# A gated cross-attention and expert program on one core: the 16-head attention's input made in the cross-attention's tail, with one scale for both norms

## The reference

```
x = x + tanh(g_ffn[0])   * L0_ffn(layernorm(x))            # experts: adds per tile
x = x + tanh(g_xattn[1]) * L1_xattn(layernorm(x), ctx)     # rms_norm of q and k
x = x + tanh(g_ffn[1])   * L1_ffn(layernorm(x))

def L1_ffn(x):                                  # x is the LayerNorm of the rows
    h = x * rsqrt(mean(x*x) + 1e-6) * ln1_w     # a second norm on top of it
    q, k, v = h @ wq, h @ wk, h @ wv            # 16 heads of 128
    x = x + softmax(causal(q k^T / sqrt(128))) v @ wo
    ...
```

## Time and profile before

| | |
|---|---|
| median of three runs | 819.42 us |
| profiled execution | 822.67 us, span 820.9 us |
| mean granted clock of TensorE | 0.963 |
| busy, share of the span | PE 93%, PEld 76%, DVE 52%, ACT 43%, POOL 28% |
| chain that ended last | PE 81%, ACT 6%, DVE 4%, DMA 3%, POOL 2%, issue 2% |

### The profile page before, as it was taken

The page is one execution under the profiler, slowest core; times in us unless marked ns, Lnnn a source line. Parts: engine busy times, 40 slices in busy tenths (PEclk is TensorE's granted clock), DMA queues, the critical chain, the costliest instruction groups (busy, mean ns, idle before and its releaser), DMA issues.

```text
span 820.9 us, 13560 instructions
## 1 busy us (share of the span) xinstructions
PE 761.7 (93%) x4626; PEld 621.6 (76%) x4627; DVE 430.3 (52%) x831; ACT 352.7 (43%) x852; POOL 231.1 (28%) x284
## 2 busy tenths in 40 slices
PE   7998899999849985999999999999898999999996
PEld 5887755666537863898898898898686888888885
DVE  6688262111446876345445435436545566656564
ACT  3887302222137874445445455455542233333332
POOL 5110040000355425221321321310423334343430
PEclk9999789999968998999999999999989999999999
DMA  8960031111100002101100110000113334343421
GB/s 318 420 232 2 1 103 46 45 46 37 53 19 2 2 2 76 41 20 34 45 26 32 34 36 32 25 14 1 58 39 91 98 109 118 105 122 101 130 74 51
DMA packets 25670, 58.29 MB, mean 71 GB/s; under 512 B 3600, under 2 KB 14480, under 8 KB 24352
## 3 DMA queue, kind: packets, MB, share of 16 engines
q1 hardware_dynamic: 24864, 55.68, 21.0%
q0 software_dynamic: 768, 2.10, 0.8%
HBM read 51.67 MB, written 6.09 MB: 70 GB/s over the span
## 4 chain that ended last, share of the span: by engine, by line
PE 81%; ACT 6%; DVE 4%; DMA 3%; POOL 2%; issue 2%; POOLq 0%; SPq 0%; PEldq 0%; ACTq 0%; PEld 0%; DVEq 0%
PE PS L329 15%; PE PS L331 15%; PE PS L330 15%; PE PS L1374 7%; PE PS L1099 6%; PE PS L1114 3%; PE PS L441 3%; PE PS L432 2%; PE PS L399 2%; PE PS L405 2%; PE PS L1380 2%; ACT x_probT L523 1%; PE PS L387 1%; ACT x_prob L552 1%; PE PS L454 1%
## 5 line engine op out<-in xcount | busy, mean ns | idle before, releaser
L329 PE MATMUL PS<-tTh,wh 128*128 128x512 f32 x200 | 79.9, 399 | 0.0
L889 ACT ACTIVATE hhh<-hh 128x512 fp32r<-128x512 f32 x50 | 31.6, 632 | 112.2 <-DVE hh L915 100.6
L330 PE MATMUL PS<-tTl,wh 128*128 128x512 f32 x200 | 79.3, 397 | 0.0
L331 PE MATMUL PS<-tTh,wl 128*128 128x512 f32 x200 | 79.3, 397 | 0.0
L513 DVE TENSOR_TENSOR hhl<-hh,hhh 128x512 fp32r<-128x512 f32 x50 | 52.6, 1052 | 34.9 <-ACT hhh L889 34.9
L1481 ACT ACTIVATE sm<-sm,nmx 128x128 f32<-128x128 f32 x128 | 49.7, 391 | 37.5 <-DVE nmx L1538 37.5
L971 POOL TENSOR_TENSOR wl<-wraw,wh 128x512 fp32r<-128x512 f32 (+1 forms) x50 | 58.2, 1163 | 8.4 <-POOL wh L969 7.9
L513 DVE TENSOR_TENSOR oTl<-PS,oTh 128x512 fp32r<-128x512 f32 x32 | 22.1, 692 | 71.6 <-ACT oTh L1475 71.6
L969 POOL CAST wh<-wraw 128x512 fp32r<-128x512 f32 (+1 forms) x50 | 26.1, 521 | 118.2 <-PE PS L331 113.3
L1577 POOL CAST ah<-araw 128x512 fp32r<-128x512 f32 (+1 forms) x32 | 16.6, 518 | 145.0 <-PE PS L331 143.1
L1099 PE MATMUL PS<-WE,xsT 128*128 x120 | 56.4, 594 | 0.1
(11 more groups left out here) (241 smaller groups left out, 1848.4 us busy)
## 6 DMA issues: line engine op xcount, KB each, us to landing
WE<-moe SPq DMA_DIRECT2D x8, 1536.0 KB, 13.8
wraw<-moe SPq DMA_DIRECT2D x25, 384.0 KB, 3.1
araw<-attn SPq DMA_DIRECT2D x16, 384.0 KB, 3.1
cwb<-cw_d SPq DMA_DIRECT2D x20, 256.0 KB, 3.8
...
```

What stands on the lines that cost most here:

```text
L329: nc.tensor.matmul(out, wh_, xh_, start=first, stop=False, **kw)
L330: nc.tensor.matmul(out, wh_, xl_, start=False, stop=False, **kw)
L331: return nc.tensor.matmul(out, wl_, xh_, start=False, stop=last, **kw)
L889: nc.scalar.activation(hhh[half][:, :], hh[half][:, :], ACT.Copy).then_inc(s.hi_done, 1)
```

## The change

The two norms become one scale. With v the variance of a row, LayerNorm and RMSNorm together give (x - mean) divided by the root of v (1 + 1e-6) + 1e-6 x 1e-5. VectorE makes that number per tile (`input_moments`) for tiles 0 to 5, 6 and 7, GpSimd its power (`input_power`), VectorE scales X straight into FX (`input_rows`), and the weight ln1, now laid along partitions, is applied where ScalarE writes tTh and VectorE tTl (`input_high`, `input_low`, two operations of 128x128 each). tT is not written there. The turns use the four banks of the scores once they are free.

These pieces go into steps 6 to 8 of the cross-attention; the barrier between the two stages is gone, and so are the fillers and the squares. The weights of the attention have SBUF of their own now, beside the cross-attention's, and are loaded once the experts' last product is done; head 0's are split by GpSimd in the tail. The first projections and value products come in another order. Z is made by GpSimd, all eight tiles behind the split for head 1.

At the opening of cross-attention 1 the query biases move ahead of the key products of the expert stage, the ln3 power of tiles 0 and 1 goes between the fourth and sixth gathers, VectorE writes the normalised rows 0 and 1 between the last adds of expert rows, and ScalarE masks keys 0 and 1.

The diff, cut (constants, semaphores, the other buffers that move with araw, the copies of the ring's new order, the barriers of the other engines and the host's packing of ln1 are left out):

```diff
...
+        araw = [sb(f"araw{i}", [P, 3 * D], where=l1) for i in range(2)]
...
                     scores(n + 1)
                 if has(n - 1):
                     values_columns(n - 1)
+                if L and n == B:
+                    input_turn(pe, MOST)
...
                         values(n)
                     if has(n + 2):
                         query_squares(n + 2)
+                    if n == B - 1:
+                        for b in range(4):
+                            input_turn(pe, b)
                     if has(n):
                         values_back(n)
+                    if n == B - 1:
+                        for b in range(4, MOST):
+                            input_turn(pe, b)
...
 
             act.wait_ge(bias_done, 1 + L)
             if L:
+
+                for b in range(2):
+                    act.wait_ge(Es.kt_free, b + 1)
+                    for odd in range(2):
+                        m = nc.scalar.activation(m_.k2T[b][:, :, odd, :], K1[:, b, :].rearrange("p (c s) -> p c s", c=C), ACT.Copy, scale=pair_rows[:, odd:odd + 1])
+                    m.then_inc(s.keys_done, 1)
                 key_columns(act, MOST, B)
...
                     copy("oT", n, m_.oT[:, :, :].rearrange("p k s -> p (k s)"), 4 * S)
                 if has(n + 2):
                     queries(n + 2)
+                if L and n == B - 1:
+                    input_high(act, 0)
+                    input_high(act, 1)
                 if has(n) and L:
                     copy("oT", n, m_.oT[:, :, :].rearrange("p k s -> p (k s)"), 4 * S)
                 if has(n + 1):
                     exps(n + 1, 1)
                 if has(n + 3):
                     columns("xT", n + 3, m_.xT)
-            if L:
-                squares_act(act, z_done, 0, MOST)
+                if L and n >= B - 1:
+                    for b in ((2, 3), (4, 5, 6, 7))[n - B + 1]:
+                        input_high(act, b)
...
+        def input_moments(ch, k):
+
+
+            b0, b1 = INPUTS[k]
+            for b in range(b0, b1):
+                i = nc.vector.bn_aggr(mv[:, b, :], st[:, b, :])
+            ch.link(i)
+            nc.vector.tensor_scalar(in_ms[:, b0:b1].unsqueeze(2), mv[:, b0:b1, 1:2], 1.0 + RMS_EPS, RMS_EPS * LN_EPS, ALU.mult, ALU.add).then_inc(in_stats, 1)
+
+        def input_power(pool, k):
+            b0, b1 = INPUTS[k]
+            pool.wait_ge(in_stats, k + 1)
+            nc.gpsimd.tensor_tensor(in_rstd[:, b0:b1], in_ms[:, b0:b1], mhalf[:, b0:b1], ALU.pow).then_inc(in_power_done, 1)
+
+        def input_rows(dve, b):
+            dve.wait_ge(in_power_done, 1 + [b0 <= b < b1 for b0, b1 in INPUTS].index(True))
+            nc.vector.tensor_scalar(FX[:, b, :], X[:, b, :], mv[:, b, 0:1], in_rstd[:, b:b + 1], ALU.subtract, ALU.mult).then_inc(n_done, 1)
+
+        def input_turn(pe, b):
+            pe.wait_ge(n_done, b + 1)
+            if b < 4:
+                pe.wait_ge(xs[1].sub_done, 2 * B)
+            else:
+                pe.wait_ge(tlo_done, b - 3)
+            for c in range(C):
+                m = nc.tensor.transpose(PS[:, b % 4, c * P:(c + 1) * P], FX[:, b, c * P:(c + 1) * P], ident[:, :])
+            m.then_inc(t_done, 1)
+
+        def input_high(act, b):
+            act.wait_ge(t_done, b + 1)
+            for c in range(C):
+                m = nc.scalar.activation(tTh[:, c, b * S:(b + 1) * S], PS[:, b % 4, c * P:(c + 1) * P], ACT.Copy, scale=col("ln1", c))
+            m.then_inc(thi_done, 1)
+
+        def input_low(dve, b):
+            dve.wait_ge(thi_done, b + 1)
+            for c in range(C):
+                m = nc.vector.scalar_tensor_tensor(out=tTl[:, c, b * S:(b + 1) * S], in0=PS[:, b % 4, c * P:(c + 1) * P], scalar=col("ln1", c),
+                                                   in1=tTh[:, c, b * S:(b + 1) * S].bitcast(F32), op0=ALU.mult, op1=ALU.subtract)
+            m.then_inc(tlo_done, 1)
...
             for n in steps():
                 if has(n + 1):
                     softmax(n + 1, 0)
                 if has(n - 1):
                     output(n - 1)
+                if L and n == B - 1:
+                    input_low(dve, 0)
+                    input_low(dve, 1)
...
                 if has(n):
                     normalise(n)
+                if L and n == MOST:
+                    for b in range(MOST):
+                        input_rows(dve, b)
                 if L and n == B - 1:
-                    powered(dve, "ln4")
-                    for b in range(MOST):
-                        ln_scale(Z[:, b, :], X[:, b, :], b).then_inc(z_done, 1)
+                    input_rows(dve, MOST)
+                    for b in range(2, MOST):
+                        input_low(dve, b)
+                if L and n == B:
+                    input_rows(dve, B - 1)
+                    nc.vector.tensor_scalar(ms[:, :].unsqueeze(2), mv[:, :, 1:2], LN_EPS, None, ALU.add).then_inc(stats_done, 1)
+                    input_low(dve, MOST)
+                    input_low(dve, B - 1)
 
...
-            power(pool, "ln1" if L == 0 else "ln3", 0)
-            normed(0)
-            normed(1)
-            power(pool, "ln1" if L == 0 else "ln3", (EARLY, FIRST)[L])
-            if L:
-                masked_keys(0)
-                masked_keys(1)
+            if L == 0:
+                power(pool, "ln1")
+                normed(0)
+                normed(1)
+                power(pool, "ln1", EARLY)
+            else:
+                power(pool, "ln3", FIRST)
+                pool.wait_ge(s.ln_done, FIRST)
...
+            v.tensor_tensor(scaled_bq[:, :], cols[:, 2, :], cols[:, 3, :], ALU.mult).then_inc(bias_done, 1)
+            v.tensor_scalar(vec("bo1"), vec("bo1"), tg[:, 1:2], None, ALU.mult).then_inc(xs[1].bo_scaled, 1)
...
@@ -1310,6 +1387,8 @@
                 nc.gpsimd.indirect_dma_start(FX[:, b, :], None, ys_d, bass.IndirectOffsetOnAxis(pos[:, b:b + 1], 0)).then_inc(s.gathered[b], 16)
                 if b == FIRST:
                     keys_power(MOST, B, 2)
+                if b == FIRST + 2:
+                    power(pool, "ln3")
...
-            def first_queries():
-                pe.wait_ge(tlo_done, B // 2)
-                pe.wait_ge(aw_split, 2)
-                proj(0, 0, 0, 0, 0)
-
-            columns_pe(pe, gxn, n_done, t_done, tlo_done, first_queries)
-            fill(4, 3)
+
+            pe.wait_ge(aw_split, 2)
+            pe.wait_ge(tlo_done, B // 2 + 1)
+            proj(0, 0, 0, 0, 0)
+            pe.wait_ge(tlo_done, B // 2 + 2)
+            proj(0, 0, 1, 0, 1)
+            input_turn(pe, B - 1)
+            pe.wait_ge(av_split, 2)
+            pe.wait_ge(tlo_done, B - 1)
+            values(0, 2)
             pe.wait_ge(tlo_done, B)
-            for i, (which, half) in enumerate(((0, 1), (1, 0), (1, 1))):
-                proj(0, 0, which, half, i + 1)
+            values(1, 3)
+            pe.wait_ge(ring_act, 1)
+            proj(0, 0, 0, 1, 4)
+            pe.wait_ge(ring_dve, 1)
+            proj(0, 0, 1, 1, 5)
+            pe.wait_ge(ring_act, 2)
+            values(2, 6)
+            pe.wait_ge(ring_act, 3)
+            values(3, 7)
+
+            pe.wait_ge(xs[1].dve_free, sum(r == "D" for _, _, r in turns[1]))
+            pe.wait_ge(xs[1].act_free, sum(r == "A" for _, _, r in turns[1]))
             open_acc()
-            pe.wait_ge(av_split, 2)
-            for k in range(4):
-
-                pe.wait_ge((ring_act, ring_dve)[k // 2], k % 2 + 1)
-                values(k, 4 + k)
             head(0, 0, 1, True)
...
+            input_power(pool, 0)
             head(0, 0, 0, True, 0)
+            input_power(pool, 1)
+            input_power(pool, 2)
+            power(pool, "ln4")
+            pool.wait_ge(xs[1].dve_free, reads_no[1]["O", B - 1])
             nc.gpsimd.memset(causal[:, :], 0.0).then_inc(const_done, 1)
             pool.wait_ge(const_done, 4)
             nc.gpsimd.affine_select(out=causal[:, :], in_=causal[:, :], compare_op=ALU.is_ge, fill=NEG, base=0,
                                     pattern=[[-1, S]], channel_multiplier=1).then_inc(const_done, 1)
             head(1, 1, 0, True, 1)
+            powered(pool, "ln4")
+            for b in range(B):
+                ln_scale(Z[:, b, :], X[:, b, :], b, nc.gpsimd).then_inc(z_done, 1)
...
+            sp.wait_ge(Es.d_done, SLOTS)
             load(0, attn_d[0])
             load_values(0)
             load(1, attn_d[1])
@@ -1648,9 +1747,8 @@
...
-            power(pool, "ln4")
-            power(pool, "rms1")
+            attn_pool(pool)
             barrier(pool, 2)
-            power(pool, "ln4", MOST)
...
             ffn_act(act)
             xattn_act(act, 1)
-            barrier(act, 2)
-
-            def last_squares(b):
-                if b == 2:
-                    squares_act(act, z_done, MOST, B)
-                if b == 4:
-                    act.wait_ge(squared, B)
-
-            columns_act(act, t_done, thi_done, last_squares)
             attn_act(act)
```

(20 more changed lines are left out.)

67 lines of the change are left out of this document (34 added, 33 removed).

## The result

| | before | after |
|---|---|---|
| runs shown, median | 819.42 us | 807.9 us (805.57 to 810.02) |
| ratio | | 0.986, 95% interval 0.983 to 0.989 |
| profiled execution, span | 822.67, 820.9 us | 806.14, 804.4 us |
| mean granted clock | 0.963 | 0.972 |

The forecast was 807.8 us, with a range from 803.8 to 812.5. The median lies within 0.1 us of it, which is closer than the spread of the runs can confirm. The two profiled spans differ by 16.5 us and the medians by 11.5, so the profiles cannot simply be subtracted.

What follows compares the result with a forecast made beforehand. Bounds: TensorE inside the head loop; before it, chains of waits at the second cross-attention's opening and end. 1.6 + 11.7 - 1.65 = 11.65 us off the median 819.4 gives 807.8 us, range 803.8 to 812.5.

Steps and rivals of the forecast that it cites:

- Opening, 1.6: Opening of the second cross-attention: first turn no longer waits for ScalarE's key copies, at 230.1 not 231.70; gain 1.6 us.
- in the bounds: Opening of the second cross-attention: gain only 0.6 us if the attention-weight loads hold the gathers by 1 us more.
- Tail, 11.7: End of the second cross-attention: turning the inputs there brings the first head from 338.60 to 326.9; gain 11.7 us.
- The term for FX's stretch: Tail: FX's six scales on VectorE alternate with GpSimd's splits, sixth row at 308.2 not 305.3; priced at 0.4 us.
- The clock's rival: Tail: projections and values spend 6 us of work at the lower clock, costing 6 us: 813.8 us; chance 0.15.
- also in pieces: Clock from 300 to 312 in the kernel before: 1.00 although TensorE worked in pieces, set against 0.50 from 230 to 240.
- Behind it, -1.65: Behind the tail, at the first heads: Z's eight scales on GpSimd delay head 0's softmax norms; loss 1.65 us.
- Norm 0, two inputs in SBUF, waits for 345.8: Head 0's softmax on VectorE: norm 0 waits until a Z scale on GpSimd ends at 345.8, itself ending at 346.3.
- just fits: GpSimd behind Z's scales: head 2's first split ends at 352.8 and TensorE wants it at 352.68.

Runs made afterwards that it cites:

- tail only: The changed kernel with the opening of the second cross-attention put back as it was: 810.3 us, ratio 0.9878 to the kernel before.
- opening only: The kernel before with only the changed opening of the second cross-attention: 817.39 us, ratio 0.9969 to the kernel before.
- Z late: The changed kernel with Z's eight scales on GpSimd behind head 15's split instead of head 1's: 807.88 us, ratio 0.9849 to the kernel before.
- Z twice: The changed kernel with GpSimd writing each of Z's eight rows twice behind head 1's split: 817.55 us, ratio 0.9978 to the kernel before.
- the second profile: The changed kernel measured again without any edit: 808.55 us, ratio 0.9865 to the kernel before.
- both forms: FX's rows by tensor_scalar in the changed kernel, or by scalar_tensor_tensor in a variant of it: 808.49 us in one run of the variant.

## Why the prediction was right, and where it wasn't

Counted from tile 5's output (298.57 in the forecast's frame):

| mark | forecast | measured |
|---|---|---|
| six FX scales done | 9.6 | 8.7 |
| copy oT of tile 7 | 10.3 | 10.28 |
| two low parts done | 12.0 | 11.05 |
| tile 7 normalised | 12.7 | 12.35 |
| output 7 read | 15.6 | 15.74 |
| row 7 done | 18.0 | 18.17 |
| first value product | 18.8 | 18.91 |
| first head | 28.3 | 28.61 |

*Opening, 1.6.* Right as the edits' own effect on the first turn (1.62). The power pushed add 6 by 0.74 us, as forecast; the loads pushed it by another 0.3 and took 0.3 back, which I had only in the bounds. ScalarE's keys were hidden, as said. But I stopped counting at the first turn, and 0.5 to 1.0 us more were gained between it and tile 5's output.

*Tail, 11.7.* Measured 11.42 and 10.94. The order of the chain was as forecast, every mark within 1 us. The term for FX's stretch was right in kind (4.07 and 2.02 us) and nearly right in weight: off the path, 0 instead of 0.4. Its premise, that VectorE ends about 0.3 us behind a split, was read from two rows of which only gxn shows it (321.83 against 321.55); nmx ended within 0.02 us of its split, and FX's rows ended 0.15 behind. A low part took 0.57 (0.60 forecast), a high part 0.57 (0.6). Two errors met: VectorE was ready for output 7 0.7 us before the forecast's 15.6 and waited 0.80 for it, since TensorE took 1.91 and not 1.03. The clock's rival was put down as 0.15 for 6 us. As a mechanism it is there in each profile of the new tail without fillers, at 1.1 to 1.6 us where the order of the tail is unchanged (tail only: 2.7, with 30.24 against 27.52), so its chance was too low and its size too high. I had argued that the end of the cross-attention, "also in pieces", had kept 1.00 before; but that was one profile, and in opening only, with the same old tail, output 6 came 9.51 us behind tile 5's and the clock was 0.83 from 300 to 310.

*Behind it, -1.65.* This step failed: "Norm 0, two inputs in SBUF, waits for 345.8". I had carried over to GpSimd's tensor_scalar what the rows showed for its copy and its subtraction. Norms beside Z scales took 0.86 and 0.69 us and delayed no product. The loss was 0.42 us, by TensorE's wait for the split, and Z late won 0.5. The rest of the step, that head 2's split "just fits", was right to a quarter of a microsecond, as Z twice shows. It missed the 0.24 us by which the fifth scale ran longer while VectorE's norm 1 and the copy of the keys behind it ran.

*The sum.* 11.65 forecast; the stretches give 1.34 + 0.51 + 11.42 - 0.42 = 12.85 or, by the second profile, 1.34 + 1.04 + 10.94 - 0.42 = 12.9, and the medians 11.5 and 10.8 with an interval of 2.5 and more either way. The failed step made the sum 1.2 us too small and the uncounted part of the opening another 0.5 to 1.0; the loads and the clock made it too large by 0.5 to 1.0. That the median came out at 807.9 is therefore partly luck.

*GpSimd beside VectorE.* By the Trainium skill's page GPSIMD Engine Reference, section Engine selection, an operation with one tensor input runs on GpSimd at about line rate. The trace still disagrees: 1.21 to 1.24 us a scale against VectorE's 0.34. By the Trainium skill's page SBUF — State Buffer, section Who interferes with whom, an operation of VectorE in a 2-port mode, or with two inputs in SBUF against one of GpSimd that reads SBUF, and the GpSimd operation exclude each other for the whole instruction. The six scales agree in both forms (2.02 became 4.07; about 2.8, six times 0.47, became 4.67, and five rows of six ended right behind a split's instruction). Norm 0, with two inputs in SBUF, doesn't: it began and ended within one scale.
